# Expert tiles handled two at a time in a routed decoder layer, with the row turns one pair ahead

## The reference, cut to what matters

```python
gates = top-2 of softmax(xn @ Wg.T), renormalised          # 4096 tokens, 16 experts
for e in range(16):
    h = silu(xn @ W1[e]) * (xn @ W3[e])                    # 256 -> 176
    out = out + gates[:, e:e+1] * (h @ W2[e])              # 176 -> 256
x = x + out
```

## Time and profile before

| | us |
|---|---|
| median of 3 runs | 808.99 (808.33 to 810.88) |
| profiled execution | 809.31 |
| its span, first to last instruction | 807.5 |
| TensorE matmuls busy | 789.9 |
| VectorE / ScalarE / GpSimd busy | 592.1 / 435.1 / 393.6 |

### The profile page before, as it was taken

One profiled execution on the slowest core, in us unless ns is written; L12 is line 12 of the kernel. 1 busy time (PEld: TensorE's weight loads), 2 busy tenths in 40 slices (PEclk: granted clock), 3 DMA queues, 4 the chain that ended last, 5 costly groups with the idle time before them and its releaser, 6 DMA issues. The chain is left out here.

```text
span 807.5 us, 20968 instructions
## 1 busy us (share of the span) xinstructions
PE 789.9 (98%) x5911; PEld 750.1 (93%) x5912; DVE 592.1 (73%) x1720; ACT 435.1 (54%) x1193; POOL 393.6 (49%) x560
## 2 busy tenths in 40 slices
PE   9999999999999999999999999999999999999995
PEld 8899999999999999999999999999897899999994
DVE  4757777888787878878887878778767566666663
ACT  4473554637273554547372644546255377767773
POOL 2432134443545344544445344544436368687886
PEclk9999999999999999999999999999999999999998
DMA  9786673755747392846657382849779458777780
GB/s 270 255 285 235 211 263 102 268 178 191 246 162 272 108 314 82 286 147 220 217 173 263 127 306 91 294 135 346 253 299 353 138 107 132 121 127 130 132 140 2
DMA packets 105962, 161.19 MB, mean 200 GB/s; under 512 B 10705, under 2 KB 69649, under 8 KB 105041
## 3 DMA queue, kind: packets, MB, share of 16 engines
q1 hardware_dynamic: 80544, 132.89, 48.0%
q0 software_dynamic: 14800, 17.61, 11.9%
q10 hardware_dynamic: 10576, 10.19, 4.9%
HBM read 50.14 MB, written 112.47 MB: 201 GB/s over the span
## 5 line engine op out<-in xcount | busy, mean ns | idle before, releaser
L799 POOL DMA_INDIRECT out<-narrow,sidx x79 | 122.8, 1554 | 45.4 <-DVE sidx L2043 23.3
L1274 ACT ACTIVATE xn3T<-ps 128x512 f32<-128x512 f32 (+1 forms) x18 | 10.3, 574 | 140.4 <-PE ps L819 135.9
L808 PE MATMUL ps<-w_hi,fT_hi 128*128 128x256 f32 x256 | 79.8, 312 | 0.2
L1339 ACT ACTIVATE phi<-ps,nmax 128x128 f32<-128x128 f32 x256 | 73.5, 380 | 8.1 <-DVE nmax L1745 7.9
L1601 DVE TENSOR_TENSOR fT_lo<-relu_v,fT_hi 128x512 fp32r<-128x512 f32 x64 | 51.1, 798 | 32.3 <-ACT relu_v L1353 32.3
L808 PE MATMUL ps<-w_hi,fT_lo 128*128 128x256 f32 x256 | 72.3, 282 | 0.0
L808 PE MATMUL ps<-w_lo,fT_hi 128*128 128x256 f32 x256 | 72.1, 282 | 0.0
L1353 ACT ACTIVATE relu_v<-ps,b_sb 128x256 f32<-128x256 f32 x128 | 68.9, 538 | 0.0
L1352 ACT ACTIVATE fT_hi<-ps,b_sb 128x256 fp32r<-128x256 f32 x128 | 67.9, 530 | 1.0 <-PE ps L808 1.0
L808 PE MATMUL ps<-hT_hi,w_hi 128*128 128x256 f32 x256 | 67.1, 284 | 0.0
L808 PE MATMUL ps<-hT_hi,w_lo 128*128 128x256 f32 x256 | 66.9, 283 | 0.0
(11 more groups left out here) (330 smaller groups left out, 2715.1 us busy)
## 6 DMA issues: line engine op xcount, KB each, us to landing
expert_rows<-zero_rows SPq DMA_DIRECT2D x16, 4352.0 KB, 16.2
narrow<-expert_rows ACTq DMA_DIRECT2D x71, 136.0 KB
expert_up_hi<-X SPq DMA_DIRECT2D x16, 352.0 KB, 2.8
e_hi<-expert_up_hi SPq DMA_DIRECT2D x2, 2816.0 KB, 10.1
part_raw<-in_E SPq DMA_DIRECT2D x30, 176.0 KB
expert_up_lo<-part_raw SPq DMA_DIRECT2D x15, 352.0 KB, 3.1
e_lo<-expert_up_lo SPq DMA_DIRECT2D x2, 2464.0 KB, 13.0
X<-in_x SPq DMA_DIRECT2D x16, 256.0 KB
```

The costliest lines, as they stand in the source:

```text
L799: pool.indirect_dma_start(out_rows, bass.IndirectOffsetOnAxis(sidx[:, u:u + 1], 0), yg[:, u, :], None, bounds_check=NT * P - 1, oob_is_err ...
L808: return pe.matmul(out_, lhsT, rhs, start=start, stop=stop)
L1274: return act.activation(out_, in_, ACT.Copy)
L1339: last = act.activation(phi[:, g, h, :], ps[:, g, h * M:(h + 1) * M], ACT.Exp, bias=nmax[:, g, h:h + 1])
```

## The change

TensorE, ScalarE and VectorE go through the expert tiles in pairs (s, s+1). In a pair TensorE runs `turn_rows(s+4)`, `turn_rows(s+5)`, `turn_hidden(s)`, `turn_hidden(s+1)`, `up(s+2)`, `up(s+3)`, `down(s)`, `down(s+1)`. ScalarE runs `tile_of(s+6)`, `tile_of(s+7)`, `rows_hi(s+4)`, `rows_hi(s+5)`, `hidden_hi(s)`, `hidden_hi(s+1)`, `load_rows(s+6)`, `load_rows(s+7)`, `gate_half(s+2)`, `gate_half(s+3)`, `rows_out(s)`, `rows_out(s+1)`. The turned rows get four buffers in place of two. `up` and `down` wait for both parts of their input at their start. The tiles' edges are turned and compared before `up(0)`. SyncE and GpSimd keep their programs. The loop runs over the same 16 tiles a pass.

```diff
+        def in_pairs(step, eng, begin=None):
+            for u in range(0, GB, 2):
+                step(u, u, 2, False)
+            with eng.Fori(0, (SLOT_TILES // GB - 2) // 2) as g:
...
+                for u in range(0, 2 * GB, 2):
+                    step(g * 2 * GB + (GB + u), u % GB, 2, False)
...
+            for u in range(0, LEFT, 2):
+                step(SURE + u, u, min(2, LEFT - u), True)
+        def those_from(s, u, ahead, last):
+            return [(s + n, (u + n) % GB) for n in range(ahead, ahead + 2) if not (last and u + n >= LEFT)]
             def turn_rows(s, u):
+                if not (isinstance(s, int) and s < 2):
+                    pe.wait_ge(xgT_ready, s - 1)
                 pe.wait_ge(rows_loaded[u], (s - u) * PER + 16)
...
-                pe.wait_ge(xgT_hi, s + 1)
+                pe.wait_ge(xgT_ready, s + 1)
...
-                pe.wait_ge(hidT_hi, s + 1)
+                pe.wait_ge(hidT_ready, s + 1)
...
             turn_rows(1, 1)
+            pe.wait_ge(edges_loaded, 16 * 2)
...
             up(0, 0)
+            up(1, 1)
+            turn_rows(2, 2)
+            turn_rows(3, 3)
+            def two_tiles(s, u, n, last):                     # TensorE
+                for v in those_from(s, u, 4, last):
+                    turn_rows(*v)
+                for k in range(n):
+                    turn_hidden(s + k, u + k)
+                for v in those_from(s, u, 2, last):
+                    up(*v)
...
+                for k in range(n):
+                    down(s + k, u + k)
...
+            def two_tiles(s, u, n, last):                     # ScalarE
+                loads = [] if first(s) else [(s + k, (u + k) % GB) for k in (GB - 2, GB - 1)
+                                             if not (last and u + k >= LEFT)]
+                tiles = [tile_of(v[0]) for v in loads]
+                for v in those_from(s, u, 4, last):
+                    rows_hi(*v)
+                for k in range(n):
+                    hidden_hi(s + k, u + k)
+                for v, tile in zip(loads, tiles):
+                    load_rows(*v, tile)
+                for v in those_from(s, u, 2, last):
+                    gate_half(*v)
+                for k in range(n):
+                    rows_out(s + k, u + k)
```

More of the change, by code:

```diff
@@ L271, in decoder @@
         hidT = tuple(sb(f"hidT_{part}", [P, 2, 2, P], F32R)[:, :, :, :] for part in ("hi", "lo"))
-        xgT = tuple(sb(f"xgT_{part}", [P, 2, DC, P], F32R)[:, :, :, :] for part in ("hi", "lo"))
+        xgT = tuple(sb(f"xgT_{part}", [P, 4, DC, P], F32R)[:, :, :, :] for part in ("hi", "lo"))
         ps = stack.enter_context(nc.psum_tensor("ps", [P, 8, 512], F32))
@@ L386, in in_groups @@
                 step(SURE + u, u, True)
+        def in_pairs(step, eng, begin=None):
+            for u in range(0, GB, 2):
+                step(u, u, 2, False)
+            with eng.Fori(0, (SLOT_TILES // GB - 2) // 2) as g:
+                if begin is not None:
+                    begin()
+                for u in range(0, 2 * GB, 2):
+                    step(g * 2 * GB + (GB + u), u % GB, 2, False)
+            if begin is not None:
+                begin()
+            for u in range(0, LEFT, 2):
+                step(SURE + u, u, min(2, LEFT - u), True)
+        def those_from(s, u, ahead, last):
+            return [(s + n, (u + n) % GB) for n in range(ahead, ahead + 2) if not (last and u + n >= LEFT)]
         def first(n):
@@ L1207, in part @@
                 def part(x_part, w, c, start, stop):
-                    return mm(ps[:, 2 + u % 2, 0:2 * INTER], xgT[x_part][:, u % 2, c, :],
+                    return mm(ps[:, 2 + u % 2, 0:2 * INTER], xgT[x_part][:, u % 4, c, :],
                               w[:, bass.ds(e, 1), :].rearrange("p e i -> p (e i)"), start, stop)
-                pe.wait_ge(xgT_hi, s + 1)
+                pe.wait_ge(xgT_ready, s + 1)
                 for c in range(DC):
@@ L1214, in up @@
                     part(0, e13_lo[c], c, False, False)
-                pe.wait_ge(xgT_ready, s + 1)
                 for c in range(DC):
@@ L1239, in down @@
                 part(0, 1, e2b, LO + IR, False, False)
-                pe.wait_ge(hidT_ready, s + 1)
                 part(1, 0, e2a[0], P, False, False)
@@ L1246, in _ @@
             turn_rows(1, 1)
+            pe.wait_ge(edges_loaded, 16 * 2)
+            for o in range(2):
+                last_mm = mm(ps[0:1, 7, o * P:(1 + o) * P], edge[:, o, D:D + 1], ident[:, :])
+            last_mm.then_inc(edge_ps, 1)
             up(0, 0)
[L1249 to L1255, removed]
-                    pe.wait_ge(edges_read, 1)
[L1257 to L1268, removed]
+            up(1, 1)
[8 more added lines that the diff above has]
+                    up(*v)
+                if first(s):
+                    pe.wait_ge(e2_loaded, 16 * 3)
+                    pe.wait_ge(edges_read, 1)
+                for k in range(n):
+                    down(s + k, u + k)
+            in_pairs(two_tiles, pe, expert_at.clear)
         @block.scalar
@@ L1514, in rows_hi @@
                 act.wait_ge(xgT_ps, s + 1)
-                copy(xgT[0][:, u % 2], ps[:, u % 2, 0:D].rearrange("p (c s) -> p c s", c=DC)).then_inc(xgT_hi, 1)
+                copy(xgT[0][:, u % 4], ps[:, u % 2, 0:D].rearrange("p (c s) -> p c s", c=DC)).then_inc(xgT_hi, 1)
             def tile_of(s):
@@ L1550, in _ @@
             gate_half(0, 0)
[L1552 to L1566, removed]
+            gate_half(1, 1)
+            rows_hi(2, 2)
+            rows_hi(3, 3)
+            def two_tiles(s, u, n, last):
[12 more added lines that the diff above has]
+                    rows_out(s + k, u + k)
+            in_pairs(two_tiles, act)
             for u in range(GB):
@@ L2003, in edge_rows @@
                 dve.wait_ge(edge_ps, 1)
-                dve.tensor_copy(edge_row[:, :, :], ps[0:1, 1, 2 * P:4 * P].rearrange("p (o t) -> p o t", o=2)[:, :, 0:SLOT_TILES])\
+                dve.tensor_copy(edge_row[:, :, :], ps[0:1, 7, 0:2 * P].rearrange("p (o t) -> p o t", o=2)[:, :, 0:SLOT_TILES])\
                     .then_inc(edges_read, 1)
@@ L2024, in rows_in @@
                 dve.wait_ge(xgT_hi, s + 1)
-                dve.tensor_tensor(xgT[1][:, u % 2], ps[:, u % 2, 0:D].rearrange("p (c s) -> p c s", c=DC),
-                                  xgT[0][:, u % 2].bitcast(F32), ALU.subtract).then_inc(xgT_ready, 1)
+                dve.tensor_tensor(xgT[1][:, u % 4], ps[:, u % 2, 0:D].rearrange("p (c s) -> p c s", c=DC),
+                                  xgT[0][:, u % 4].bitcast(F32), ALU.subtract).then_inc(xgT_ready, 1)
             def product(s, u):
@@ L2048, in _, with two_tiles @@
             rows_in(1, 1)
+            edge_rows()
+            meeting_tiles()
+            numbers_of_tiles()
             product(0, 0)
[L2051 to L2061, removed]
+            product(1, 1)
+            rows_in(2, 2)
+            rows_in(3, 3)
+            def two_tiles(s, u, n, last):
+                for v in those_from(s, u, 4, last):
+                    rows_in(*v)
+                for k in range(n):
+                    hidden_in(s + k, u + k)
+                for k in range(n):
+                    scatter_index(s + k, u + k)
+                for v in those_from(s, u, 2, last):
+                    product(*v)
+            in_pairs(two_tiles, dve)
 def kernel(**inputs):
```

## The result

The changed kernel takes 849.06 us (median of 4 runs, 846.20 to 851.37) against 809.31 for the kernel before (808.33 to 810.88): a ratio of 1.0476, 95% interval 1.0447 to 1.0504. It is slower by 40 us. The forecast was 831, 18 us too low. 849 lies in the whole range stated (813.6 to 852), but outside the forecast's own, 820 to 843.

The account below looks back on a forecast made before the run. TensorE, busy 98% of the span, was taken to bound the kernel. 809.3 + 19.6 (35 ring turns of 0.56) + 2.2 (start) = 831.1, stated as 831 us; whole range 813.6 to 852, the forecast's own 820 to 843.

Parts of the forecast that it names:

- the start: Ahead of the expert loop: TensorE waits for both edge gathers before up(0), near 638.0; costs 2.2 us, bounds 1.2 and 3.
- TensorE's stream: TensorE's work per pair stays 4.02 us; fewer switches between transposes and products gain nothing; waits for xgT_lo and hidT_lo are free.
- The ring: Load lands, rows turned, hidden turned, ScalarE issues next load: 4.65 us a pair against 4.09, 35 turns, 19.6 us.
- The landing: Second load of a pair, from issue to rows there: 2.6 us, bounds 2.1 and 3.3.
- a phase fixed by the ring: Reason given for the landing: a pair's second scatter begins about 0.6 us before the second load's issue, its traffic overlapping.
- The rival with the long landing: Two loads together under the scatters land in 3.3 us: ring 5.35, 44 us more, time 855; chance 0.09.
- The queues beside the ring: ScalarE's tile_of reads (0.8 us a pair), TensorE's expert_of (0.30) and GpSimd's scatters all stay hidden.
- The end: Last slots: two short stalls become one longer, scatters follow as before; 0, within 0.5 us.
- The lead: Kernel before: table loads have five slots (10 us) of lead, and no view shows TensorE waiting for one.
- 0.02 for half of the stage: Clock rival: idling TensorE granted 1.2 GHz for half of the expert stage, 39 pairs 2 us longer, 910; chance 0.02.

Follow-up runs that it names:

- experiment 2: Changed kernel with each pair in the order hidden turns, up, row turns, down, the other two engines in step; 820.30 us, ratio 1.0136.
- experiment 5: experiment 2, with TensorE also reading the expert numbers of tiles s+4 and s+5 ahead of both down; 824.85 us, ratio 1.0161.
- experiment 11: Changed kernel with row turns behind up, edges behind turn_rows(3), expert numbers read ahead of down except in a loop pass's first pair; 817.35 us.
- experiment 3: Changed kernel with every scatter index out of bounds, so that scatters run but write no row; 831.76 us, ratio 1.0289.
- experiment 9: Changed kernel with ScalarE issuing a pair's two loads ahead of rows_hi and hidden_hi, TensorE and VectorE as they were; 868.81 us, ratio 1.0733.
- experiment 1: Changed kernel with turn_hidden ahead of turn_rows in each pair, ScalarE and VectorE in step, loads right behind hidden_hi; 841.44 us, ratio 1.0375.
- Experiment 7: Changed kernel with only the turn and comparison of the edges moved behind turn_rows(3); 843.04 us, ratio 1.0396.
- experiment 4: Kernel before, tile by tile, with slot s loading tile s+4 in place of s+7; 869.52 us, ratio 1.0728.
- experiment 8: Kernel before, with slot s loading tile s+5 in place of s+7; 814.25 us, ratio 1.0044.

## Why the prediction was right, and what it mis-sized

The direction and the mechanism were as predicted; the size was 18 us short in the medians, 20.3 in the profiled executions (after's is the slowest of its four). At the marks of the result section the forecast had 0, +2.9, +19.6 and -0.7: its 2.2 for the start count work, and by the first product of tile 4 or of tile 74 the new order has done 0.66 us of turns more than the old. Measured: +1.3, +5.1, +35.3 and +0.4. Its terms, one by one:

- **TensorE's stream, 4.02 a pair.** Right: where nothing stalls (experiments 2, 5, 11) pairs of 3.98 to 4.02 occur. Turning in pairs gains nothing that can be measured. The waits for `xgT_lo` and `hidT_lo` were free in the stage.
- **The ring.** Right in kind. From the landing of one second load to the issue of the next first load, 34 turns of after: 1.39 in the median, 1.49 in the mean (forecast 1.38). First to second load 0.66 (0.67). TensorE idles once a pair between the two row turns, released by the table's DMA, as the forecast said. The pairs were 5.11 apart where it had said 4.6 to 4.7.
- **The landing, the step that failed in size.** I took 2.6; the second load landed in 2.90 in the mean of the 34 turns, from 2.3 to 4.6. It wasn't the ring that made it long: in experiment 2, where nobody waits for it, it is 3.1. That is 0.30 x 34 = 10.2 us. The 2.6 wasn't wrong for before, whose 71 loads from tile 8 on landed in 2.60 in the mean (by the last completion in the trace); I had seen both kinds and put the ring nearer the short one. In every kernel in pairs that scatters, the second of the two loads took 2.84 to 3.09 in the mean behind tile 9's, whether anybody waited for it or not. So the reason that I gave, a phase fixed by the ring, isn't what these runs show. Most of the time over 2.3 is the scatters' traffic: with it gone the same load lands in 2.33, median (experiment 3). By the Trainium skill's page "DMA: Bandwidth & Descriptors", section "Anatomy of one DMA — SWDGE (gpsimd) path", the estimate was 2.3 and the forecast 821; experiment 3's loads without scatter traffic agree with it, those of after don't, and the measurement decides. That section is on the GpSimd path, while these loads are issued by ScalarE, so what agrees is the size and not a path that it describes. First loads of a pair landed in 2.58, mean.
- **The rest of the 35.3 us in the 35 pairs, where the forecast had 19.6.** The issue was 0.10 later in the mean: 3.5 us. The first turn took 7.33 in place of 4.65, since tile 9's load landed after 4.65 us: 2.7. The pairs of before were 4.10, where I had subtracted 4.09: -0.5. With the landing these make 15.9, against 35.3 - 19.6 = 15.7. The two stretches at half clock that lie in the pairs (3.4 us at most) are inside these terms, not beside them.
- **The rival with the long landing** (2.05 + 3.3, 855 us) came nearer in its total than the forecast: 6 us off, against 18. In mechanism the landing lies between the two, 2.90 by 2.6 and 3.3.
- **The queues beside the ring.** `tile_of` and `expert_of` were hidden as said, in after. I saw that `tile_of` would be late next in a ring of 4.3 or less, but not that the queue's path closes into a ring of its own. Experiment 9 shows it, and that my picture of one ring couldn't predict an edit to the other. Experiments 1, 5 and 9 all missed in the same way: each cut the link I looked at, and time came up in the queue of an engine that I had not worked out with the edit in place.
- **The start.** Predicted +2.2, `up(0)` near 638.0. It started at 639.05, which is 637.7 on before's scale (its loads are issued 1.3 later). The way to tile 4 was 5.1 longer, where the forecast's 2.2 make 2.9 at this mark, and its upper bound 3 makes 3.7: outside the bounds. What I had left out are the clock (below), which made `up(0)` and `up(1)` take 3.43 us in place of 1.94, so 1.5, and a wait for a buffer of transposes: `turn_rows(4)` stood 0.79 for `xgT_lo` of tile 2. The clock's part isn't the same in each execution: experiment 3 has the same program up to there, kept the clock, and was 3.8 longer than before. Experiment 7 prices the placement of the edges at 6.0 us in all: more than the start, since the first turns and the clock go with it.
- **The end.** 0 predicted, which is -0.7 from the first product of tile 74 on; 0.4 measured, so 1.1 more. No run tells why.
- **The lead.** I wrote of five slots, 10 us, of lead before. From the issue within its slot to the turn it is less, 7.3 us by the same timelines. Nothing in the sum used it. Experiments 4 and 8 show where it begins to count: five tiles ahead costs 3 us, four costs 59.

## What to carry to other kernels

Before batching steps, follow each transfer from its issue to its use through all the queues it stands in: if its issue waits, over any engine, for work that comes after its use, it is a closed ring, and the ring's length is the pace. Price a landing by the traffic that lies beside it after the change, and not by the mean of the kernel before: two loads issued together landed later here than one a slot did. When one ring is cut, work out the next longest with the edit in place, register reads and DMA issues included, before calling a stall removed.

## What the runs showed of the hardware that was not expected

**The clock in short idle stretches.** The start of after, in TensorE's timeline, and two windows of it:

```profile
638.38 0.70 PE L826 MATMUL ps<-ident,narrow 128*1 128x128 f32 x4 [2.32 <-DMA narrow<-expert_rows,edge_i]
639.05 0.65 PE L826 MATMUL ps<-e_hi,xgT_hi 128*128 x1
...
643.87 0.77 PE L1221 MATMUL ps<-ident,narrow 128*128 128x128 f32 x4 [0.79 <-DVE xgT_lo L2048]
...
655.37 0.41 PE L1221 MATMUL ps<-ident,narrow 128*128 128x128 f32 x2 [2.76 <-DMA narrow<-expert_rows]
```

```profile
638.30:642.40 4.10, 4.02 (x16) 3.61 (x17) 1.90 (x9) 0.32 (x1) 0.00 (x0) 0.58 0.38 106
655.80:659.20 3.40, 3.40 (x14) 3.40 (x13) 1.76 (x7) 1.42 (x4) 2.47 (x2) 0.50 0.29 63
```

After idling 2.32 us TensorE was granted 0.58 in the mean, mostly its lower level of 1.2 GHz, while its products came 0.29 apart in place of 0.16. After 2.76 us of idling it fell to 0.50 for 3.4 us, 655.8 to 659.2, and once more from 703.6 on, behind the late load of tile 27 (0.53 and 1.74 idle in a row). The common stalls of about 1 us left the clock at 1.00. Idling of like length didn't always end in this: 2.18 us ahead of `up(0)` in experiment 2 and 2.25 in experiment 9 left it at 1.00, and experiment 4 was granted 0.50 for 3.4 us from 669.0 on without a stall over 1.4 us in the stage before it. I had given this 0.02 for half of the stage; it came in three short stretches.

**Landings of 4 us and more.** Tiles 9 (issued 650.58) and 27 (698.68) landed after 4.65 and 4.57 us, all others of the stage in 2.0 to 3.6. It isn't the scatters' traffic: with no row written (experiment 3) the median fell to 2.33, and three second loads still took 4.0 to 4.1. Nor is it a loop's edge in TensorE's program: pairs 2 and 20 issued them, the loop begins with pair 8 and its second pass with pair 24. The DMA table has something beside each of the two: a packet on the instruction queue q8.

```profile
q8 instruction: 1, 0.02, 1.3%
```

That is 650.5 to 655.3; 698.6 to 703.3 has one too. It holds over all 13 traces of this case. Of their 923 loads from tile 8 on, 78 had such a packet (16 KB, around 1 us) beside them at some time before they landed. All 16 loads that took over 3.9 us are among these 78, and their median is 3.08; the other 845 have a median of 2.52 and a longest of 3.7. So the long landings go together with these packets. Whether the packets delay the loads wasn't tried, and stays open.

**A read of a register in a queue** took 0.28 us on ScalarE and 0.30 on TensorE (medians), plus the instructions around it: in experiment 9's chain `rows_hi` comes behind two reads and two issues of loads, 2.0 us after the first read began. Moving the same reads in experiment 5 was worth 0.10 us a pair away from the loop's edges and cost 0.83 in each edge pair (5.57 against 4.74).
